# The first self attention: ScalarE seeds the score banks with the negated maximum, PE adds three products

## The reference, cut to what matters

```
h = layernorm(x)
q = (h @ wq).reshape(B, S, 16, 64); k, v likewise
attn = softmax(einsum("bihd,bjhd->bhij", q, k) * 64 ** -0.5)
out = einsum("bhij,bjhd->bihd", attn, v).reshape(B, S, 1024)
x = out @ wo + bo + x
```

## Time and profile before

| | |
|---|---|
| median of 3 runs | 1968.06 us (1966.6 to 1968.89) |
| profiled execution, its own time | 1968.18 us |
| its span | 1966.3 us |
| the stage that changes | from about 35 to 857 us |
| PE busy | 1784.3 us (91%) |
| VectorE busy | 1143.7 us (58%) |
| ScalarE busy | 794.2 us (40%) |
| GpSimd busy | 923.3 us (47%) |
| mean granted PE clock | 0.96 |

### The profile page before, as it was taken

How to read it: one execution, slowest core, us unless ns; L and a number is a source line. 1 busy time by engine, 2 the same in 40 slices (tenths; PEclk the granted TensorE clock), 3 DMA queues, 4 the chain that set the end, 5 groups by cost and what they waited for, 6 DMA issues and landing times. The chain is left out here.

```text
span 1966.3 us, 29515 instructions
## 1 busy us (share of the span) xinstructions
PE 1784.3 (91%) x10124; PEld 1118.4 (57%) x10124; DVE 1143.7 (58%) x2101; ACT 794.2 (40%) x1315; POOL 923.3 (47%) x807
## 2 busy tenths in 40 slices
PE   3799999999999999979999989996899886898799
PEld 2455555555555555557555768884444435565678
DVE  4566666666666666524566343346788834686601
ACT  3244444444444444412444233221466671354340
POOL 1267777777777777840122200201356554466010
PEclk9799999999999999989999989996899988899999
DMA  1000000000000000040000010102344420000101
GB/s 54 6 4 7 4 6 3 6 3 6 3 6 3 6 3 1 1 120 25 1 1 1 1 35 22 33 12 45 69 81 82 75 40 23 9 1 1 33 15 43
DMA packets 49824, 43.69 MB, mean 22 GB/s; under 512 B 18304, under 2 KB 44444, under 8 KB 49727
## 3 DMA queue, kind: packets, MB, share of 16 engines
q1 hardware_dynamic: 45375, 35.86, 8.2%
q0 software_dynamic: 4352, 6.56, 1.6%
HBM read 22.84 MB, written 2.24 MB: 13 GB/s over the span
## 5 line engine op out<-in xcount | busy, mean ns | idle before, releaser
L1224 POOL TENSOR_TENSOR x<-x,sa_p_buf 128x1024 f32<-128x1024 f32 x192 | 456.2, 2376 | 149.5 <-ACT sa_p_buf L1055 139.0
L1136 DVE TENSOR_REDUCE sa_mx<-sa_front 128x1 f32<-128x512 f32 x512 | 328.8, 686 | 153.9 <-PE sa_front L934 153.2
L1055 ACT ACTIVATE sa_p_buf<-sa_score 128x512 f32<-128x512 f32 x512 | 276.0, 597 | 314.2 <-PE sa_score L984 295.2
L997 PE MATMUL sa_out<-sa_p_buf,sa_v_buf 128*64 128x512 f32 x1024 | 246.2, 602 | 0.0
L1716 POOL TENSOR_TENSOR x<-x,bias_out 128x1024 f32<-128x1024 f32 x24 | 55.7, 2350 | 267.5 <-POOLq L1901 152.0
L528 ACT ACTIVATE sa_p_buf<-sa_score 128x1024 f32<-128x1024 f32 (+1 forms) x160 | 141.1, 937 | 89.2 <-PE sa_score L476 89.1
L342 DVE TENSOR_REDUCE sa_mx<-sa_front 128x1 f32<-128x512 f32 (+1 forms) x256 | 155.9, 650 | 24.7 <-PE sa_front L283 21.8
L934 PE MATMUL sa_front<-sa_k_hi,sa_q_hi 64*128 64x512 f32 x512 | 129.6, 502 | 10.7 <-DVE sa_mx L1136 9.3
L1605 POOL TENSOR_TENSOR ca_probs<-ca_s_sb,ca_inv 128x616 f32<-128x616 f32 x64 | 77.9, 1218 | 127.4 <-DVE ca_inv L1539 127.4
L934 PEld LDWEIGHTS sa_front<-sa_k_hi,sa_q_hi 64*128 64x128 f32 x512 | 48.4, 185 | 149.2 <-issue 50.8
L997 PEld LDWEIGHTS sa_out<-sa_p_buf,sa_v_buf 128*64 128x64 f32 x1024 | 65.0, 136 | 115.4 <-issue 84.9
(11 more groups left out here) (188 smaller groups left out, 3332.9 us busy)
## 6 DMA issues: line engine op xcount, KB each, us to landing
x<-in_x SPq DMA_DIRECT2D x8, 512.0 KB, 7.7
sa_q_stack<-sa_hi SPq DMA_DIRECT2D x64, 64.0 KB, 2.3
sa_k_stack<-sa_hi SPq DMA_DIRECT2D x64, 64.0 KB, 2.4
sa_m_rows<-sa_m_turned SPq DMA_DIRECT2D x128, 2.0 KB
ff_w<-in_L_xattn_ff_w SPq DMA_DIRECT2D x16, 128.0 KB, 2.1
sa_k_top<-sa_hi POOLq DMA_DIRECT2D x32, 64.0 KB, 2.6
sa_q_top<-sa_hi POOLq DMA_DIRECT2D x32, 64.0 KB, 2.6
sa_q_stack<-sa_lo SPq DMA_DIRECT2D x32, 64.0 KB, 2.4
```

The costliest lines, as they stand in the source:

```text
L997: mm = pe.matmul(out_ps[64 * j:64 * j + 64, :], v_buf[:, b, kt, 64 * j:64 * j + 64], p_buf[:, s % NPB, j, :], start=(kt == 0), stop=(kt == ...
L1055: nc.scalar.activation(p_buf[:, s % NPB, j, :], score_ps[n % NSCORE][:], ACT.Exp, scale=SCALE).then_inc(exp_done, 1)
L1136: dve.tensor_reduce(mx[:, b, j, qt, half:half + 1], front_ps[bank(item, j)][:], AX.X, ALU.max).then_inc(drained, 1)
L1224: nc.gpsimd.tensor_tensor(acc[:, h], prev, cur, ALU.add).then_inc(added, 1)
```

## The change

The negated maximum is no longer added by a matmul. VectorE negates the turned maxima in one operation, SP writes them to DRAM (`m_line`) and, when that has landed, reads them back spread over all 128 partitions (`m_all`, 512 KB). ScalarE copies `m_all` into the two banks of a step (`seed`, 128x1024 SBUF to PSUM), and the three products of each head are added on top (`start=False`). The score banks are now two tensors of two banks, and the exponent of both heads is one instruction of 128x1024. ScalarE's order in a unit: both exponents, the seed of the next unit's first step, the high parts or sums, the seed of its second step. `one_rows` and the clearing of `m_rows` go; four matmuls at the start of the stage write each score bank once (`primed`). The turn of unit 6 (and of unit 3 in the first pass) is moved ahead of the unit's m's (`leads`, `behind`), on PE and on VectorE.

```diff
-        6: [("n", ("m", 4, 0)), ("n", ("m", 5, 0)), ("n", ("t", 0))],
+        6: [("n", ("t", 0)), ("n", ("m", 4, 0)), ("n", ("m", 5, 0))],
...
-        3: [("n", ("m", 0, 0)), ("n", ("m", 1, 0)), ("c", ("t", 1)), ("n", ("q", 1))],
+        3: [("c", ("t", 1)), ("n", ("m", 0, 0)), ("n", ("m", 1, 0)), ("n", ("q", 1))],
...
-        score_ps = [ps(f"score{i}", [P, HALF]) for i in range(NSCORE)]
+        score_ps = [ps(f"score{i}", [P, G, HALF]) for i in range(NSCORE // G)]
...
                     sp.wait_ge(drained, drained_count(g, b, ("t", h)))
-                    for j in range(G):
-                        for part in range(2):
-                            row = j * dh + part
-                            sp.dma_start(m_rows[row:row + 1, b, h * HALF:(h + 1) * HALF].bitcast(F32),
-                                         m_turned[j * QH:(j + 1) * QH, part, :].bitcast(F32)).then_inc(max_in, DMA)
+                    sp.dma_start(m_line[h], m_turned[:]).then_inc(max_out, DMA)
+                    sp.wait_ge(max_out, lin(g, b, DMA * HALVES, DMA * (h + 1)))
+                    sp.dma_start(m_all[:, h, :], m_line[h:h + 1].rearrange("o r n -> o (r n)").to_broadcast(
+                        (P, G * HALF))).then_inc(max_in, DMA)
...
                 def scores(g, b, s):
...
+                    pe.wait_ge(seeded, lin(g, b, TILES, (s + 1) * G))
                     keys, queries = slice(kt * P, (kt + 1) * P), slice(h * HALF, (h + 1) * HALF)
                     for part, (ks, qs) in enumerate(((k_hi, q_hi), (k_hi, q_lo), (k_lo, q_hi))):
                         for j in range(G):
                             r = slice(dh * j, dh * j + dh)
-                            pe.matmul(score_ps[(s * G + j) % NSCORE][:], ks[r, b, keys], qs[r, b, queries], start=(part == 0),
-                                      stop=False, skip_group_check=True)
-                    for j in range(G):
-                        r = slice(dh * j, dh * j + dh)
-                        pe.matmul(score_ps[(s * G + j) % NSCORE][:], one_rows[r, :], m_rows[r, b, queries], start=False,
-                                  stop=True, skip_group_check=True).then_inc(score_full, 1)
+                            mm = pe.matmul(score_ps[s % len(score_ps)][:, j, :], ks[r, b, keys], qs[r, b, queries], start=False,
+                                           stop=(part == 2), skip_group_check=True)
+                            if part == 2:
+                                mm.then_inc(score_full, 1)
...
                 def front():
+                    for n in range(NSCORE):
+                        pe.matmul(score_ps[n // G][:, n % G, :], ident[:], hT[:, 0, 0:HALF], start=True, stop=True).then_inc(primed, 1)
...
                 def both(g, b):
                     for u in range(UNITS):
+                        for of, item in leads(u, g, b):
+                            front_item(*of, item)
...
-                    for j in range(G):
-                        n = s * G + j
-                        act.wait_ge(score_full, lin(g, b, TILES, n + 1))
-                        nc.scalar.activation(p_buf[:, s % NPB, j, :], score_ps[n % NSCORE][:], ACT.Exp,
-                                             scale=SCALE).then_inc(exp_done, 1)
+                    act.wait_ge(score_full, lin(g, b, TILES, (s + 1) * G))
+                    nc.scalar.activation(p_buf[:, s % NPB], score_ps[s % len(score_ps)][:], ACT.Exp,
+                                         scale=SCALE).then_inc(exp_done, G)
+
+                def seed(g, b, s):
...
+                    h, kt = divmod(s, KT)
+                    if kt == 0:
+                        act.wait_ge(max_in, lin(g, b, DMA * HALVES, DMA * (h + 1)))
+                    if not (is_first(g, b) and s * G < NSCORE):
+                        act.wait_ge(exp_done, lin(g, b, TILES, s * G - NSCORE + G))
+                    nc.scalar.activation(score_ps[s % len(score_ps)][:], m_all[:, h, :].rearrange("p (j n) -> p j n", j=G),
+                                         ACT.Identity).then_inc(seeded, G)
...
+                        for n in coming[:1]:
+                            seed(*n)
                         for of, item in owned(u, g, b, ("q", "k", "den")):
                             if item[0] == "den":
                                 take_sums(*of, item[1])
                             else:
                                 high(*of, item)
+                        for n in coming[1:]:
+                            seed(*n)
...
-                        rows = fr[0:G * QH, 0:P]
-                        dve.tensor_scalar(m_turned[:, 0, :], rows, -1.0, None, ALU.mult).then_inc(m_high, 1)
-                        dve.wait_ge(m_high, lin(g, b, HALVES, item[1] + 1))
-                        dve.scalar_tensor_tensor(out=m_turned[:, 1, :], in0=rows, scalar=-1.0,
-                                                 in1=m_turned[:, 0, :].bitcast(F32), op0=ALU.mult,
-                                                 op1=ALU.subtract).then_inc(drained, 1)
+                        dve.tensor_scalar(m_turned[:], fr[0:G * QH, 0:P], -1.0, None, ALU.mult).then_inc(drained, 1)
...
-                        for of, item in owned(u, g, b, "m"):
+                        for of, item in leads(u, g, b) + owned(u, g, b, "m"):
                             front_item(*of, item)
```

More of the change, by code:

```diff
@@ L769, in owned, with behind, leads @@
                 if item[0] in kinds and owner(who, g, b) is not None]
+    def behind(u, g, b):
+        kinds = ("q", "k", "v", "den")
+        return owned(u, g, b, kinds if leads(u, g, b) else kinds + ("t",))
+    def leads(u, g, b):
+        return owned(u, g, b, ("t",)) if lanes_of(g, b)[u][0][1][0] == "t" else []
     def sums(s):
@@ L821, in wide_attention @@
         drained = sem("drained")
-        max_in = sem("max_in")
-        joined, m_high = sem("joined"), sem("m_high")
+        max_out, max_in = sem("max_out"), sem("max_in")
+        joined = sem("joined")
         score_full = sem("score_full")
@@ L843, in wide_attention @@
         NPROJ = 4
-        NMAX = 2 * G
         with nc.Block() as block:
@@ L1015, in both @@
                             front_item(*of, item)
-                        for of, item in owned(u, g, b, ("q", "k", "v", "t", "den")):
+                        for of, item in behind(u, g, b):
                             front_item(*of, item)
@@ L1074, in front @@
                         split_h(c)
-                    nc.scalar.activation(one_rows[:].rearrange("p (r n) -> p r n", r=2),
-                                         ones[:].unsqueeze(1).to_broadcast((P, 2, 64)), ACT.Identity,
-                                         scale=0.0).then_inc(ones_set, 1)
-                    act.wait_ge(ones_set, 1)
-                    for j in range(G):
-                        r = slice(dh * j, dh * j + 2)
-                        ins = nc.scalar.activation(one_rows[r, :].rearrange("p (r n) -> p r n", r=2),
-                                                   ones[r, :].unsqueeze(1).to_broadcast((2, 2, 64)), ACT.Identity)
-                    ins.then_inc(ones_set, 1)
                     for item in first_front:
                         high(0, 0, item)
+                    act.wait_ge(primed, NSCORE)
+                    seed(0, 0, 0)
+                    seed(0, 0, 1)
                 def both(g, b):
@@ L1094, in both @@
                         exponent(g, b, 2 * u + 1)
+                        if u < UNITS - 1:
+                            coming = [(g, b, 2 * u + 2), (g, b, 2 * u + 3)]
+                        elif not is_last(g, b):
+                            coming = [(*after(g, b), 0), (*after(g, b), 1)]
+                        else:
+                            coming = []
+                        for n in coming[:1]:
+                            seed(*n)
                         for of, item in owned(u, g, b, ("q", "k", "den")):
@@ L1141, in front_item @@
                         if not (is_first(g, b) and item[1] == 0):
-                            dve.wait_ge(max_in, lin(g, b, DMA * NMAX * HALVES, DMA * NMAX * item[1]))
+                            dve.wait_ge(max_out, lin(g, b, DMA * HALVES, DMA * item[1]))
                         dve.wait_ge(front_full, filled_count(g, b, item))
-                        rows = fr[0:G * QH, 0:P]
-                        dve.tensor_scalar(m_turned[:, 0, :], rows, -1.0, None, ALU.mult).then_inc(m_high, 1)
-                        dve.wait_ge(m_high, lin(g, b, HALVES, item[1] + 1))
-                        dve.scalar_tensor_tensor(out=m_turned[:, 1, :], in0=rows, scalar=-1.0,
-                                                 in1=m_turned[:, 0, :].bitcast(F32), op0=ALU.mult,
-                                                 op1=ALU.subtract).then_inc(drained, 1)
+                        dve.tensor_scalar(m_turned[:], fr[0:G * QH, 0:P], -1.0, None, ALU.mult).then_inc(drained, 1)
                 def join(g, b, h, count):
@@ L1180, in both @@
```

(5 more changed lines are left out.)

21 lines of the change are left out of this document (4 added, 17 removed).

## The result

| | before | after |
|---|---|---|
| median | 1967.5 us (1966.6 to 1968.9, 4 runs) | 1945.3 us (1938.8 to 1953.3, 4 runs) |
| ratio | | 0.988 (95% interval 0.986 to 0.991) |
| profiled execution, its own time | 1968.2 us | 1953.3 us |
| its span | 1966.3 us | 1951.6 us |
| end of the changed stage in the trace | 857.1 us | 836.1 us |

The forecast was 1948 us, in a range from 1936 to 1962. The end of the stage is the table load that opens the next stage on ScalarE's timeline.

The account below looks back on a forecast made before the run. PE's own sequence was taken to bound the stage, with VectorE's round trip a second limit at the edge. 1968.2 - 21 - 1 - 0.4 + 3 = 1948.8, with half a microsecond for the clock 1948 us; range 1936 to 1962.

Parts of the forecast that it names:

- The bound and the price of a pair: Changed stage: PE's own sequence sets the time; each removed matmul pair is worth 0.23 us, 59 us for 256.
- The swallowed pair: First score step of seven of eight units: removing its pair gives nothing, as the next maximum matmuls wait for VectorE.
- m to m: From one query tile's maximum matmul pair to the next on PE: 1.28 us, VectorE's round trip, unchanged by the edit.
- Unit 7: Last two steps of a pass, with three maximum matmul pairs spaced by VectorE's reductions: no gain, still 7.0 us.
- the 0.19: Unit 1: the turn needs the joined maximum, so it can start only 0.19 us sooner, not 0.47.
- By coincidence just the time that PE needs: Between a unit's two maximum matmul pairs: VectorE's 1.28 us round trip about equals PE's own 1.27 us before the change.
- The seed at 1.02 us: ScalarE's 128x1024 copy of maxima into score banks takes 1.02 us, within bounds 0.8 and 1.5.
- The chain: ScalarE's exponents and seeds before the next scores: fits with nothing over in unit 6; cost 0, up to 0.5 a pass.
- Rival B: ScalarE's seeds dearer than SBUF activations: 1955 to 1962 us at 1.3 us, 2037 at 2.0; chances 0.12 gaining, 0.05 slower.
- The DMA: Maxima to DRAM (1.7 us) and back as 512 KB (4.3 us): hidden behind other work in the repeated passes.
- Start and end: Stage's edges: 3 us lost at the start, 1 gained in the first pass, 0.4 in the last, half for the clock.
- rival C: PE's clock falls in new 0.2 us gaps: gain gone below 0.967 granted, 1987 us at 0.94; chance 0.05.

Follow-up runs that it names:

- the new order: Changed kernel with PE doing maximum matmuls, two score steps, then maximum matmuls in units with two maximum pairs, except unit 6: 1921.1 us, 0.975 of the kernel before.
- the second trace: The changed kernel run once more with nothing altered: 1944.2 us (6 runs), ratio 0.988.

## Why the prediction was right, point by point

- **The bound and the price of a pair** (PE, 0.23 us, 59 us at most, not 101): right. The score pairs are 0.23 apart wherever the granted clock is full.
- **The swallowed pair** (m to m stays 1.28): right, and shown by leaving out the fourth product alone, by halving the reductions, and by the new order. Forecast 46.9 us a pass, measured 46.94. Unit 7 takes 7.00 us (311.10 to 318.10), forecast "still 7.0". In unit 1 the turn starts at 279.13, 0.06 us behind the joined maximum (278.90 + 0.17), as the 0.19 assumed.
- **"By coincidence just the time that PE needs"**: off by 0.1 us a unit. A wait that ends in the last moment also exposes a weight load, and this was so before the change. It didn't touch the forecast, since it is the same in both kernels; but it made the new order's gain 1.8 in place of 1.15 us a pass.
- **The seed at 1.02 us**: measured 1.025. The estimate from the Trainium skill (ScalarE: Activation LUTs, What ACT_TABLE_LOAD costs), 1.04 us, lies 0.015 above. The rule of the Trainium skill (ScalarE: Activation LUTs, Step-by-step: what each stage is for) that ScalarE is faster to PSUM than to SBUF is seen at most faintly: 128x1024 from SBUF took 1.025 us into PSUM and 1.044 into SBUF, from four instructions of another output type, and the exponent, from PSUM into SBUF, took 1.026.
- **The chain**: it fitted in unit 6 to 0.05 us, as worked out. From 200 to 700 us no weight load of the scores waited for a seed. The price beyond that point was mis-sized: 0.49 us more a seed cost 0.65 us a pass, and I had put the loss of the whole 1.5 there. Of that, 0.37 came over a path that the prediction didn't have, the denominators' bank that ScalarE empties late. Rival B's last number was also added up wrongly: 53 us a pass gives 1948 + 14 x 6.1 = 2033, not 2037.
- **The DMA**: hidden, even without the early turn. To DRAM it took 1.2 us from SyncE's first issue to its second (307.24 to 308.46; taken 1.7), and the spread of 512 KB 3.6 (taken 4.3).
- **Start and end**: taken 3 us lost, less 1, 0.4 and half a microsecond gained, so 1.1 lost in all. The repeated passes gave 14 x 1.47 = 20.5 us, so the rest of the stage gained 0.5 in the first trace (21.0 in all) and lost 2.0 in the second (18.5). The forecast lies between, and two traces don't size the term. What they show of it: the turned rows were ready at 66.56 and 67.63 us, 2.3 and 1.3 sooner than assumed; the kernel before with the priming alone has its first turned rows 1.05 us sooner, so about that much is the priming, for which I had only allowed half a microsecond, and the other 1.1 of the first trace goes with the clock of that execution (full rate from 38.3 us in place of 40.9). The DMAs were shorter too, so that PE began the scores at 72.82 and 74.51 where I had said 76.2. Against that ScalarE waited 2.90 us for the second half's maxima in the first pass (100.45; 2.60 in the second trace), where I had counted a gain of 1.
- **The clock in the small gaps** (rival C): 1.00 granted from 260 to 400 us with the gaps, so this case's trace doesn't bear out the rule of the Trainium skill (TensorE: Matmul & The Clock Gate, A second HAM failure mode: psum-queue depth-cycling) at gaps of 0.2 us.

The sum was 1948.8 less 0.5. The stage gained 21.0 and 18.5 us where 20.2 was forecast (1968.2 less 1948). The medians of whole executions gained more than the stage, 22.3 us in the first comparison and 24.6 in the second. The rest was not traced; it is no more than what the half-rate time of the later stages moves single runs. So it is in part luck that the median came within 2.7 us of the forecast. The mechanism rests on the pass, 46.9 forecast and 46.94 measured.

## What to carry to other kernels

A matmul taken off the busiest engine is worth its start-to-start distance, and only where nothing else was released in the same moment; look whether the wait that would be next ends within a few hundredths of a microsecond of the start it precedes. If it does, the removal and a reordering belong together: here the removal alone gave 1.5 us a pass, the reordering alone 0.7, and both 3.3. Count a round trip through a shared bank (the end of the matmul, the reduction, the release; 1.28 us here) as a resource of its own: VectorE was busy for 68% and 69% of the stretch in the two kernels, and neither share shows it. Take a second trace before you size a term at the start of a stage.

## What the runs showed of the hardware that I had not expected

- A matmul whose release comes in the last moment costs about 0.1 us beyond the wait, as its weights are loaded in the open (0.50 us long and 0.34 to the next start, against 0.39 and 0.23).
- Four matmuls ahead of a stage changed the rate of those that followed it: 0.23 us apart in place of 0.43. They began between 34.8 and 34.9 us in every trace, but went over to the full rate at 38.3 us in one execution of a kernel and at 40.9 in another of the same.
- The same instructions in the unchanged later stages took from 1101.7 to 1115.5 us, following how long the clock was granted at half rate (103.5 to 139.5 us).
- Eight rows of 512 bytes to DRAM were there 1.2 us after the issue.
